# State-space layer with adapters: two sums of the readout handed to accumulating DMAs, the last step of softplus to VectorE

## The chip, the cores and the metric

One core of one Trainium2 chip runs the whole program. The metric is the device time of one execution in microseconds; lower is better.

## The reference

Eight samples of 256 tokens and 1,024 features pass through one layer, float32 throughout:

```python
x = x + attn(cond(x))        # cond: x W + b + 2 * (x A[slot]) B[slot], one adapter per sample
x = x + ffn(cond2(x))        # ffn: top 2 of 8 experts of rank 64
# attn, D = 2048 channels, N = 16 states
u, gate = split(h @ W_in.T)
u = silu(causal_conv4(u) + conv_b)
dt, Bm, Cm = rmsnorm of split(u @ Wx.T)           # 64, 16 and 16 wide
delta = softplus(dt @ Wdt.T + dt_bias)
state = exp(delta * A) * state + (delta * u) * Bm  # a scan over 256 tokens, per channel and state
y = sum over the 16 states of state * Cm + u * D
out = (y * silu(gate)) @ W_out.T
```

## The kernel before

The work is cut into `CHUNKS` = 128 chunks. Chunk `i` is sample `b = i // 16` and block `c = i % 16` of 128 channels; channels lie on the partitions, tokens along the free dimension. The 16 states of a chunk are taken in four quarters `q` of four states, so that one quarter is a plane of 128x1024 elements. Each engine has its own in-order program, and the engines meet at semaphores only.

For a chunk `i` the work is this:

- GpSimd forms `w = delta * u` (`weight`, 128x256) and from it the four input planes `w * Bm` (`dbu(i, q)`, 128x1024 each) into the ring `st` of state buffers, one chunk ahead of VectorE.
- ScalarE forms the four decay planes (`decay(i, q)`, four Exp of 128x255 each) in one of two PSUM tiles, `Tps[q % 2]`. It may begin one only when VectorE has multiplied the plane that was there (`mul_done`).
- VectorE scans each plane in place (`scan(i, q)`, line 1303) and multiplies it by `Cm` (`mul(i, q)`). Products 0, 2 and 3 go to `st` (line 1315). Product 1 stays in PSUM (line 1313), and `add_first` (line 1320) adds product 0 to it and writes `st`.
- GpSimd adds product 1 into product 2 (`add(i, 2)`), that into product 3 (`add(i, 3)`, both line 1538), and folds the four states of the result into two (`fold`, line 1544, 128x512).
- TensorE sums the two that are left with an identity matrix (`sum_states`, line 655) into `gbank`, VectorE adds `u * D` (`y_sum`, line 1326) and multiplies by the gate (`y_gate`, line 1331).

Beside this each chunk has up to four TensorE jobs from fixed tables: `late_job` (bank `late`: output projection of the sample before, experts), `small_job` (bank `small`: projections of `delta`, called "dt", logits and others), `half_job` (half of `gbank`: the adapter layer two samples ahead, part of the experts) and `end_job` (the first dt job of the next sample, at c = 13, in `late`). Within chunk `i` TensorE runs late job, small job, `sum_states(i-1)`, half job, end job, then waits in `ubank_free` for ScalarE's silu of the gate (`q_done`), and then runs the u projection 20 chunks ahead and the gate projection of chunk `i+1` (lines 611 and 638). A job waits until its bank was emptied. The silu waits for the three convolution taps that VectorE runs after `scan(i, 2)` (line 1284). `y_sum(i-1)` stands in VectorE's program of chunk `i`, and waits for `sum_states(i-1)` and for the half job of chunk `i`, which shares the bank.

Softplus is `relu(z) + ln(1 + exp(-|z|))` for two chunks at a time (128x512, 64 times in all). ScalarE empties the bank in two passes, Relu into `delta` (line 1016) and Abs into `tmp` (line 1017), which frees the bank; then it runs Exp and Ln on `tmp` (lines 1023, 1025); GpSimd adds `tmp` to `delta` (`delta_add`, line 1548).

Weights come in tiles of 512 KB through a ring of six buffers, issued by SyncE (line 489).

## Time and profile before

| | us |
|---|---|
| median of 3 runs (2444.42 to 2445.68) | 2444.53 |
| the profiled execution | 2442.7 |
| its span, from first to last instruction | 2440.9 |
| TensorE busy | 2240.2 (92%) |
| VectorE busy | 2229.0 (91%) |
| GpSimd busy | 2116.4 (87%) |
| ScalarE busy | 1614.2 (66%) |

"Busy" is the time in which an engine had an instruction under way. The profiled execution lies 1.8 us above its span and 1.8 us below the median. The granted TensorE clock was 0.96 of full speed over the span.

### The profile page before, as it was taken

Reading aid. Unit: us, or ns where it says so; the run is one execution under the profiler, and the core shown is the slowest. Engines: PE = TensorE matmul, PEld = TensorE weight load, DVE = VectorE, ACT = ScalarE, POOL = GpSimd, SP = SyncE. Lnnn points to the kernel's source line nnn. Section 1 sums busy time; section 2 is a strip of 40 time slices with the busy share of each in tenths; the row PEclk is TensorE's granted clock in tenths of the full one; section 3 lists DMA queues with packets and bytes.
Section 4 is the critical chain, followed back from the end, with each engine's and each line's share of the span. In section 5 each row is a group of like instructions: output and inputs, shape, how many; then the busy total and the mean of one; then the engine's idle time right before and its main releaser. Section 6 shows DMA issues by size and latency. Waiting matters only on the chain.

```text
span 2440.9 us, 30553 instructions
## 1 busy us (share of the span) xinstructions
PE 2240.2 (92%) x10140; PEld 1900.0 (78%) x10140; DVE 2229.0 (91%) x2104; ACT 1614.2 (66%) x3763; POOL 2116.4 (87%) x1090
## 2 busy tenths in 40 slices
PE   8989999999899998999989999999989977787879
PEld 7777878888678877888868887788878765666767
DVE  1389999999999999999999999999999999998892
ACT  1467667776777667776677667776677666765550
POOL 0189889999999999999899999999899999999870
PEclk9999999999999999999989998999999998989989
DMA  7454445444454444544455433644345332632342
GB/s 227 143 202 109 139 137 172 150 138 132 125 191 154 147 139 158 165 147 139 136 168 161 148 130 118 208 159 136 117 165 161 122 108 70 202 104 96 112 139 97
DMA packets 133178, 352.15 MB, mean 144 GB/s; under 512 B 38733, under 2 KB 43341, under 8 KB 131549
## 3 DMA queue, kind: packets, MB, share of 16 engines
q1 hardware_dynamic: 110254, 298.28, 37.9%
q10 hardware_dynamic: 22768, 51.93, 6.2%
q8 instruction: 81, 1.33, 0.2%
q14 instruction: 75, 0.61, 0.1%
HBM read 339.14 MB, written 11.02 MB: 143 GB/s over the span
## 4 chain that ended last, share of the span: by engine, by line
PE 42%; POOL 22%; DVE 21%; issue 9%; ACT 6%; DMA 1%; ACTq 0%; SPq 0%; DVEq 0%; POOLq 0%
POOL st L1530 12%; DVE scan L1303 11%; PE late L692 8%; PE ubank L638 7%; PE ubank L611 7%; POOL st L1538 6%; PE gbank L590 3%; DVE st L1315 3%; DVE ubank L1284 2%; PE scan L611 2%; DVE scan L1313 2%; ACT L1223 2%; POOL st L1544 2%; ACT scan L1133 2%; PE gbank L655 2%
## 5 line engine op out<-in xcount | busy, mean ns | idle before, releaser
L1530 POOL TENSOR_TENSOR st<-w_sb,bc 128x1024 f32<-128x1024 f32 x512 | 1198.0, 2357 | 122.7 <-PE gbank L655 110.3
L1303 DVE TENSOR_TENSOR_SCAN scan<-scan,st 128x1024 f32<-128x1024 f32 x512 | 1167.5, 2288 | 33.9 <-ACT scan L1133 18.4
L1133 ACT ACTIVATE scan<-delta,A_sb 128x255 f32<-128x255 f32 x2048 | 846.1, 459 | 0.1
L1538 POOL TENSOR_TENSOR st<-st 128x1024 f32<-128x1024 f32 x255 | 601.1, 2357 | 20.8 <-DVE st L1315 10.8
L611 PE MATMUL ubank<-h,wt 128*128 128x256 f32 x1712 | 423.3, 404 | 93.1 <-ACT qg L1223 87.6
L638 PE MATMUL ubank<-h,wt 128*128 128x256 f32 x2048 | 471.2, 384 | 23.2 <-ACT qg L1223 23.2
L611 PEld LDWEIGHTS ubank<-h,wt 128*128 128x128 f32 x1712 | 345.2, 204 | 161.8 <-ACT qg L1223 109.2
L638 PEld LDWEIGHTS ubank<-h,wt 128*128 128x128 f32 x2048 | 393.6, 193 | 81.7 <-ACT qg L1223 27.2
L1315 DVE TENSOR_TENSOR st<-scan,bc 128x1024 f32<-128x1024 f32 x384 | 453.8, 1208 | 0.0
L692 PE MATMUL late<-yg,wt 128*128 128x256 f32 x1792 | 407.1, 386 | 26.3 <-DVE x L1340 22.1
L1130 ACT ACTIVATE scan<-iota 128x4 f32<-128x4 f32 x512 | 86.9, 170 | 491.7 <-DVE st L1315 455.9
L692 PEld LDWEIGHTS late<-yg,wt 128*128 128x128 f32 x1792 | 347.2, 194 | 78.4 <-DVE x L1340 24.9
L1223 ACT ACT_TABLE_LOAD x128 | 164.2, 1283 | 171.9 <-DVE ubank L1284 163.7
L1548 POOL TENSOR_TENSOR delta<-delta,tmp 128x512 f32<-128x512 f32 x64 | 81.3, 1270 | 113.3 <-ACT tmp L1025 113.3
L1544 POOL TENSOR_TENSOR st<-st 128x512 f32<-128x512 f32 x127 | 161.5, 1271 | 10.0
L1137 ACT ACT_TABLE_LOAD x129 | 165.5, 1283 | 2.4
L1284 DVE SCALAR_TENSOR_TENSOR ubank<-up,cw,ubank 128x256 f32<-128x256 f32 x321 | 154.6, 482 | 9.3 <-DVE wf L1405 1.5
L1320 DVE TENSOR_TENSOR st<-scan,st 128x1024 f32<-128x1024 f32 x128 | 156.6, 1223 | 4.1
L655 PE MATMUL gbank<-st,ident 128*128 128x256 f32 x508 | 137.6, 394 | 22.5 <-POOL st L1544 16.0
L1313 DVE TENSOR_TENSOR scan<-scan,bc 128x1024 f32<-128x1024 f32 x128 | 156.2, 1220 | 0.3 <-DMA bc<-bc_rows 0.3
L590 PE MATMUL gbank<-xb,wt 128*128 128x256 f32 x672 | 153.6, 382 | 0.2 <-ACT h L976 0.2
L590 PEld LDWEIGHTS gbank<-xb,wt 128*128 128x128 f32 x672 | 128.7, 192 | 18.5 <-ACT h L976 0.6
(219 smaller groups left out, 2257.1 us busy)
## 6 DMA issues: line engine op xcount, KB each, us to landing
wt<-in_W_in SPq DMA_DIRECT2D x256, 512.0 KB, 3.6
wt<-in_W_out SPq DMA_DIRECT2D x132, 512.0 KB, 3.4
wt<-in_cond_W SPq DMA_DIRECT2D x64, 512.0 KB, 3.6
bc<-bc_rows ACTq DMA_DIRECT2D x64, 512.0 KB, 6.8
wt<-G_tiles SPq DMA_DIRECT2D x32, 512.0 KB, 3.6
wt<-in_ffn_B SPq DMA_DIRECT2D x20, 512.0 KB, 3.6
xb<-in_x SPq DMA_DIRECT2D x8, 1024.0 KB, 7.1
x<-in_x ACTq DMA_DIRECT2D x28, 256.0 KB, 4.0
```

Source lines behind the costliest of these rows:

```text
L590: mm(o, wt[:, n % W_RING, k, :], xb[:, k, :], start=(k == 0), stop=False)
L611: last = mm(o[:, 0:T], wt[:, n % W_RING, k, :], h0[:, b % 3, k, :], start=(k == 0), stop=(k == KH - 1))
L638: last = mm(ubank[:, T:2 * T], wt[:, n % W_RING, k, :], h0[:, b % 3, k, :], start=(k == 0), stop=(k == KH - 1))
L692: last = mm(o, wt[:, n % W_RING, k, :], yg[:, (NC * f + h * KH + k) % Y_RING, :], start=(h == 0 and k == 0), stop=(h == 1 and k == KH - 1))
L1133: last = fn(t[:, k, 1:T], delta[:, c, 1:T], ACT.Exp, scale=A_sb[:, col:col + 1])
L1223: fn(qg[:, i % 2, :], ubank[:, T:2 * T], ACT.Silu).then_inc(q_done, 1)
L1303: v_.tensor_tensor_scan(Tps[q % 2][:, :], Tps[q % 2][:, :], x_, 0.0, ALU.mult, ALU.add).then_inc(scan_done, 1)
L1313: v_.tensor_tensor(Tps[1][:, :], Tps[1][:, :], cq, ALU.mult).then_inc(prod_done, 1)
L1315: v_.tensor_tensor(plane(n), Tps[q % 2][:, :], cq, ALU.mult).then_inc(mul_done, 1)
L1530: tt(st[:, n % ST_RING, :, :], w_sb[:, i % 2:i % 2 + 1, :].to_broadcast([P, NQ, T]), bc[:, 0, q * NQ:(q + 1) * NQ, :], ALU.mult).then_inc( ...
L1538: tt(st[:, n % ST_RING, :, :], st[:, n % ST_RING, :, :], st[:, (n - 1) % ST_RING, :, :], ALU.add).then_inc(add_done, 1)
L1544: tt(t[:, 0:2, :], t[:, 0:2, :], t[:, 2:4, :], ALU.add).then_inc(add_done, 1)
```

## The change

The readout's sums. Product 1 goes to `st` like the others, and `add_first` and `add(i, 3)` go. In their place stand two DMAs that GpSimd issues (`add_dma`): one adds plane 0 into plane 1, the other plane 2 (which by then holds the sum of three) into plane 3. `add(i)`, the sum of plane 1 into plane 2, stays on GpSimd. The ring `st` has 8 buffers instead of 6. VectorE's order changes to scan 0, mul 0, scan 1, mul 1, scan 2, taps, mul 2, scan 3, `y_sum`, `y_gate`, mul 3.

Softplus. ScalarE runs Abs from the bank into `delta`, then Exp and Ln in place; VectorE's `delta_sum` computes `max(z, 0) + delta` from the bank in one instruction, and frees the bank. Relu on ScalarE, `delta_add` on GpSimd and the buffer `tmp` go.

For space, the matrix `sel` goes (an expert's weights are spread over partitions by two matmuls with a broadcast column of the identity, 64 partitions each, instead of one with `sel`), and `wT` shares the buffer `la`.

```diff
-ST_RING = 6
+ST_RING = 8
...
-                return mm(o, sel[:, m * P:(m + 1) * P], wT[:, :], start=True, stop=True)
+                for e in range(2):
+                    pick = ident[0:E, 2 * m + e:2 * m + e + 1].to_broadcast([E, ER])
+                    last = mm(o[e * ER:(e + 1) * ER, :], pick, wT[:, :], start=True, stop=True)
+                return last
...
+            def delta_sum(b, j):
+                job = ("dt", b, j)
+                n = 8 * b + j
+                d = delta[:, 2 * j:2 * j + 2, :].rearrange("p c t -> p (c t)")
+                dve.wait_ge(sp_step, 3 * n + 3)
+                v_.scalar_tensor_tensor(d, home(job)[:, :], 0.0, d, ALU.max, ALU.add).then_inc(delta_done, 1)
+                dve.wait_ge(delta_done, n + 1)
+                dve.sem_inc(ev_inc(job), 1)
...
                 scan(i, 0)
                 if i:
                     take_late(i - 1)
+                mul(i, 0)
                 scan(i, 1)
+                for n, j in softplus_of(i):
+                    delta_sum(n, j)
                 if i:
                     take_rest(i - 1)
-                mul(i, 0)
                 mul(i, 1)
-                add_first(i)
                 scan(i, 2)
...
+                mul(i, 2)
                 if c == 13 and b < LAST:
                     norm(b + 1)
                 scan(i, 3)
-                mul(i, 2)
-                mul(i, 3)
...
                     y_sum(i - 1)
                     y_gate(i - 1)
+                mul(i, 3)
...
             def dbu(i, q):
-                if q == 2 and i:
-                    pool.wait_ge(mul_done, 4 * i - 2)
-                if q == 1 and i >= 2:
+                if q == 3 and i >= 2:
                     pool.wait_ge(id_mm, i - 1)
...
+            def add_dma(i, k):
+                n = 4 * i + k
+                pool.wait_ge(mul_done, n + 1)
+                if k == 3:
+                    pool.wait_ge(add_done, 2 * i + 1)
+                pool.dma_start(st[:, n % ST_RING, :, :], st[:, (n - 1) % ST_RING, :, :], accum_op=ALU.add
+                               ).then_inc(acc_st[k // 2], 16)
+
+            def add(i):
+                n = 4 * i + 2
+                pool.wait_ge(acc_st[0], 16 * (i + 1))
+                pool.wait_ge(mul_done, n + 1)
...
             def fold(i):
-                pool.wait_ge(add_done, 3 * i + 2)
+                pool.wait_ge(acc_st[1], 16 * (i + 1))
...
             for i in range(CHUNKS):
-                for b, j in softplus_of(i - 1):
-                    delta_add(b, j)
-                if i + 1 < CHUNKS:
+                last = i + 1 == CHUNKS
+                if not last:
                     weight(i + 1)
-                    for q in range(3):
-                        dbu(i + 1, q)
-                add(i, 2)
-                if i + 1 < CHUNKS:
-                    add(i, 3)
-                    fold(i)
+                    dbu(i + 1, 0)
+                    dbu(i + 1, 1)
+                if i:
+                    fold(i - 1)
+                add_dma(i, 1)
+                if not last:
+                    dbu(i + 1, 2)
                     dbu(i + 1, 3)
+                add(i)
+                if not last:
+                    add_dma(i, 3)
```

The steps of the experts' softmax, which stand between these at one chunk of each sample, are left out here; they keep their order.

## Rows read from the trace of the kernel before

**Rows 1.** The page, busy time, share of the span and instructions by engine.
```profile
PE 2240.2 (92%) x10140; PEld 1900.0 (78%) x10140; DVE 2229.0 (91%) x2104; ACT 1614.2 (66%) x3763; POOL 2116.4 (87%) x1090
```

**Rows 2.** Windows: length, busy us of PE, PEld, DVE, ACT, POOL; clock; DMA.
```profile
193.00:305.00 112.00, 108.89 (x493) 94.27 (x492) 106.04 (x93) 81.83 (x195) 100.67 (x53) 0.98 0.43 122
1000.40:1194.00 193.60, 190.35 (x885) 164.77 (x884) 190.10 (x185) 133.71 (x314) 182.66 (x96) 0.99 0.47 149
1194.00:1281.60 87.60, 77.59 (x340) 64.09 (x339) 86.69 (x78) 66.20 (x154) 82.12 (x42) 0.92 0.47 154
1830.00:2106.30 276.30, 231.54 (x1001) 192.87 (x1002) 272.31 (x251) 194.29 (x448) 261.58 (x135) 0.92 0.39 127
2106.29:2227.00 120.71, 96.46 (x390) 80.24 (x389) 111.61 (x87) 80.31 (x181) 119.06 (x63) 0.90 0.36 119
```

**Rows 3.** Line 1303, the scans: ns min/median/max, first and last start; one releaser.
```profile
L1303 DVE TENSOR_TENSOR_SCAN scan<-scan,st x512: 2271/2289/2299, 119.7 to 2377.4; 128x1024 f32<-128x1024 f32 x171
...
  DVE xs L1290: 1.3, 6
```

**Rows 4.** Timeline of VectorE: start us, us, instruction.
```profile
1015.47 1.23 DVE L1313 TENSOR_TENSOR scan<-scan,bc 128x1024 f32<-128x1024 f32 x1
1016.73 1.23 DVE L1320 TENSOR_TENSOR st<-scan,st 128x1024 f32<-128x1024 f32 x1
1017.87 2.29 DVE L1303 TENSOR_TENSOR_SCAN scan<-scan,st 128x1024 f32<-128x1024 f32 x1
```

**Rows 5.** Groups of instructions: xcount, busy us, mean ns, idle before and releasers.
```profile
L1284 DVE SCALAR_TENSOR_TENSOR ubank<-up,cw,ubank 128x256 f32<-128x256 f32 x321 | 154.6, 482 | 9.3 <-DVE wf L1405 1.5 <-ACT ubank L991 0.3
L1349 DVE TENSOR_TENSOR x<-x,late 128x512 f32<-128x512 f32 x14 | 9.4, 673 | 0.0
L1016 ACT ACTIVATE delta<-small 128x512 f32<-128x512 f32 x63 | 36.3, 577 | 3.0 <-ACT hw L1095 1.5 <-issue 1.5
L1548 POOL TENSOR_TENSOR delta<-delta,tmp 128x512 f32<-128x512 f32 x64 | 81.3, 1270 | 113.3 <-ACT tmp L1025 113.3
```

**Rows 6.** Timeline of GpSimd at the start of sample 7, one chunk.
```profile
2107.36 0.73 POOL L1517 TENSOR_TENSOR w_sb<-delta,u_sb 128x256 f32<-128x256 f32 x1
2108.17 6.98 POOL L1530 TENSOR_TENSOR st<-w_sb,bc 128x1024 f32<-128x1024 f32 x3
2115.11 4.79 POOL L1538 TENSOR_TENSOR st<-st 128x1024 f32<-128x1024 f32 x2
2119.98 1.26 POOL L1544 TENSOR_TENSOR st<-st 128x512 f32<-128x512 f32 x1
2121.20 2.35 POOL L1530 TENSOR_TENSOR st<-w_sb,bc 128x1024 f32<-128x1024 f32 x1
2124.74 0.73 POOL L1517 TENSOR_TENSOR w_sb<-delta,u_sb 128x256 f32<-128x256 f32 x1
```

**Rows 7.** DMA: the SyncE queue (packets, MB, share), issues with KB and us to landing.
```profile
q1 hardware_dynamic: 110254, 298.28, 37.9%
...
wt<-in_W_in SPq DMA_DIRECT2D x256, 512.0 KB, 3.6
...
bc<-bc_rows ACTq DMA_DIRECT2D x64, 512.0 KB, 6.8
...
h<-in_x SPq DMA_DIRECT2D x1, 1024.0 KB, 6.5
```

**Rows 8.** Timeline of ScalarE's queue, three DMA issues in a row.
```profile
1240.99 1.52 ACTq L1033 DMA_DIRECT2D bc<-bc_rows  x3
```

**Rows 9.** Waits: who waited for whom, us in total, times, longest us.
```profile
POOL st L1530 <- PE gbank L655: 110.3, 49, 9.5
```

**Rows 10.** Timeline of TensorE: a heavy chunk, then c = 14 of sample 3.
```profile
1022.10 1.03 PE L655 MATMUL gbank<-st,ident 128*128 128x256 f32 x4
...
1224.25 1.13 PE L749 MATMUL late<-wT,sel 8*128 8x256 f32 x4
...
1234.51 5.17 PE L611 MATMUL ubank<-h,wt 128*128 128x256 f32 x16 [3.40 <-ACT qg L1223]
```

More of the change, by code:

```diff
@@ L219, in build @@
           A_mat, D_par, W_out, base_W, base_b, lora2_A, lora2_B, GT_all, ffn_B,
-          ident_in, mean_in, sel_in, iota_in, out):
+          ident_in, mean_in, iota_in, out):
     with ExitStack() as ctx:
@@ L376, in build @@
         scan_done = sem("scan_done")
-        prod_done = sem("prod_done")
         mul_done = sem("mul_done")
         add_done = sem("add_done")
+        acc_st = [sem(f"acc_st{i}") for i in range(2)]
         id_mm = sem("id_mm")
@@ L395, in build @@
         block = ctx.enter_context(nc.Block())
-        N_CONSTS = 12
+        N_CONSTS = 11
         SOFT_STEPS = 10
@@ L1074, in evac @@
                     ms_evac(job)
-                elif kind == "dt":
-                    dt_evac(job)
                 elif kind == "la2":
@@ L1084, in evac @@
                     act.wait_ge(*made(job))
+                    if b + 3 < B:
+                        act.wait_ge(*made(("cond", b + 3, 7)))
                     fn(wT[:, :], o[0:E, 0:T], ACT.Copy).then_inc(ev_inc(job), 1)
@@ L1177, in _ @@
                     for prev in (late_job(i - 1), small_job(i - 1), end_job(i - 1)):
-                        if prev and prev[0] not in ("wout", "wb", "B", "lg", "ms"):
+                        if prev and prev[0] not in ("wout", "wb", "B", "lg", "ms", "dt"):
                             evac(prev, i)
@@ L1311, in mul @@
                 cq = bc[:, 1, q * NQ:(q + 1) * NQ, :].rearrange("p n t -> p (n t)")
-                if q == 1:
-                    v_.tensor_tensor(Tps[1][:, :], Tps[1][:, :], cq, ALU.mult).then_inc(prod_done, 1)
-                else:
-                    v_.tensor_tensor(plane(n), Tps[q % 2][:, :], cq, ALU.mult).then_inc(mul_done, 1)
-            def add_first(i):
-                dve.wait_ge(prod_done, i + 1)
-                dve.wait_ge(mul_done, 4 * i + 1)
-                v_.tensor_tensor(plane(4 * i + 1), Tps[1][:, :], plane(4 * i), ALU.add).then_inc(mul_done, 1)
+                v_.tensor_tensor(plane(n), Tps[q % 2][:, :], cq, ALU.mult).then_inc(mul_done, 1)
             def y_sum(i):
@@ L1422, in _ @@
             norm(0)
+            delta_sum(0, 0)
+            delta_sum(0, 1)
             def take_late(i):
@@ L1459, in _ @@
                     soft_max_step(b - 1, 3)
-                add_first(i)
+                scan(i, 2)
                 if weigh:
                     soft_max_step(b - 1, 4)
-                scan(i, 2)
-                if weigh:
-                    soft_max_step(b - 1, 5)
                 if i:
@@ L1469, in _ @@
                             conv_tap(v, k)
+                if weigh:
+                    soft_max_step(b - 1, 5)
+                mul(i, 2)
                 if c == 13 and b < LAST:
@@ L1472, in _ @@
                 scan(i, 3)
-                if i == CHUNKS - 1:
-                    y_sum(i - 1)
-                    y_gate(i - 1)
-                mul(i, 2)
                 if b and c == 10:
                     soft_max_in(b - 1)
-                mul(i, 3)
-                if i and i < CHUNKS - 1:
+                if i:
                     if i == NC - 1:
@@ L1531, in dbu @@
                    bc[:, 0, q * NQ:(q + 1) * NQ, :], ALU.mult).then_inc(dbu_done, 1)
-            def add(i, k):
+            def add_dma(i, k):
                 n = 4 * i + k
+                pool.wait_ge(mul_done, n + 1)
                 if k == 3:
-                    pool.wait_ge(add_done, 3 * i + 1)
+                    pool.wait_ge(add_done, 2 * i + 1)
[4 more added lines that the diff above has]
+                pool.wait_ge(acc_st[0], 16 * (i + 1))
                 pool.wait_ge(mul_done, n + 1)
@@ L1542, in fold @@
                 t = st[:, (4 * i + 3) % ST_RING, :, :]
-                pool.wait_ge(add_done, 3 * i + 2)
+                pool.wait_ge(acc_st[1], 16 * (i + 1))
                 tt(t[:, 0:2, :], t[:, 0:2, :], t[:, 2:4, :], ALU.add).then_inc(add_done, 1)
-            def delta_add(b, j):
-                pool.wait_ge(sp_step, 2 * (8 * b + j) + 2)
-                tt(delta[:, 2 * j:2 * j + 2, :], delta[:, 2 * j:2 * j + 2, :], tmp[:, j % 2, :, :], ALU.add
-                   ).then_inc(dadd_done, 1)
-            delta_add(0, 0)
             weight(0)
-            dbu(0, 0)
-            delta_add(0, 1)
-            for q in range(1, Q):
+            for q in range(Q):
                 dbu(0, q)
             for i in range(CHUNKS):
-                for b, j in softplus_of(i - 1):
-                    delta_add(b, j)
-                if i + 1 < CHUNKS:
+                last = i + 1 == CHUNKS
+                if not last:
                     weight(i + 1)
-                    for q in range(3):
-                        dbu(i + 1, q)
-                add(i, 2)
-                if i + 1 < CHUNKS:
-                    add(i, 3)
-                    fold(i)
+                    dbu(i + 1, 0)
+                    dbu(i + 1, 1)
+                if i:
+                    fold(i - 1)
+                add_dma(i, 1)
+                if not last:
+                    dbu(i + 1, 2)
                     dbu(i + 1, 3)
+                add(i)
+                if not last:
+                    add_dma(i, 3)
 def kernel(**inputs):
```

41 lines of the change are left out of this document (14 added, 27 removed).

## The prediction

> **What bounds the kernel now.** I began with the page's busy shares [rows 1]. No engine is the bound by its average: TensorE has 92%, VectorE 91%, GpSimd 87%. So a gain must be read from each stage. The scans run from 119.7 to 2377.4 us [rows 3]; the last of them is the fourth of its chunk, some 10 us into it, so a chunk takes (2257.7 - 10) / 127 = 17.7 us on average. The windows then split the samples [rows 2]:
>
> - Chunks 1 to 11 of sample 3 (second row) stand for samples 1 to 5: 193.6 us, 17.6 a chunk, TensorE busy 190.35 (98%), VectorE 190.10 (98%). Both are full. There is no room for a gain of more than 193.6 - 190.35 = 3.3 us unless TensorE gets less work.
> - Its chunks 12 to 15 and the next chunk 0 (third row): 87.6 us, VectorE busy 86.69, TensorE 77.59. VectorE is the bound.
> - Chunks 4 to 9 of sample 0 (first row): TensorE 108.89 of 112.0, VectorE 106.04. TensorE is the bound.
> - Sample 6 (fourth row), which has no adapter layer to compute ahead: VectorE 272.31 of 276.3, TensorE 231.54. VectorE is the bound.
> - The first seven chunks of sample 7 (fifth row): GpSimd 119.06 of 120.71, VectorE 111.61. GpSimd is the bound, and one of its chunks takes 2124.74 - 2107.36 = 17.38 us [rows 6].
>
> **VectorE's part.** Product 1 and `add_first` take 1017.87 - 1015.47 = 2.40 us from start to the next scan; one product alone takes 1.14 (1017.87 - 1016.73) [rows 4]. So 1.26 us go per chunk, 161 in all. What comes is `delta_sum`, 64 times. It is not in the trace: from below, a two-operand pass over 128x512 takes 0.67; from above, two of the three-operand passes over 128x256 take 0.96 [rows 5]. I take 0.75, near the pass of equal size. It also waits for its own end before it frees the bank; the same pattern in `norm` left VectorE idle 1.3 / 6 = 0.22 us [rows 3]. So 0.97 each, 62 in all. Net, a sample of 16 chunks and 8 sums loses 20.2 - 7.8 = 12.4 us of VectorE. The new order puts a scan between a product and the decay plane that needs its PSUM tile, so ScalarE is asked for nothing sooner; ScalarE also loses one pass of 0.577 per dt job [rows 5], with 34% of idle time around it, worth nothing by itself.
>
> **GpSimd's part.** It loses one add of two, (2119.98 - 2115.11) / 2 = 2.43 us, per chunk [rows 6], and `delta_add`, 1.27 [rows 5], in half of the chunks. It gains two DMA issues. No DMA of GpSimd is in the trace, and none that accumulates. The issue: from below 0.5 us, what one costs on ScalarE's queue (1.52 / 3) [rows 8]; from above 1.27, a 128x512 pass of GpSimd. I take 1.0, nearer to the engine's own instruction, since software must build the descriptors. A chunk with a dt job is then 17.38 - 1.27 - 2.43 + 2.0 = 15.7 us, if no DMA is late.
>
> **When a DMA is late.** This decides the case. GpSimd is in order. Behind the first DMA stand two input planes, then `add`, which waits for it: cover 2 x 6.94 / 3 = 4.63 us. Behind the second stand `weight` (0.81) and two planes: cover 5.44, then `fold` [rows 6]. If both are late the cycle is add 2.43 + fold 1.22 + 2 x (issue + landing). The landing of a DMA that adds 512 KB in SBUF: from below 3.6 us, a weight tile of 512 KB; from above 6.8 (a broadcast of 512 KB), and nearly the same 6.5 for 1,024 KB [rows 7]. I work out a value between: the queue moved 298.28 MB in 37.9% of 16 engines' span, 20.1 GB/s each, so 512 KB are 1.6 us of movement and 2.0 of fixed time. An add must read both operands and write one; with reading as the limit movement is 3.25, so 5.2 us. Then the first is late by 0.6, the second is covered, and the cycle is 16.3 us, below the 17.4 to 17.7 of now. Hidden, then, but by little: the cycle reaches 17.7 when issue and landing together make 7.0, that is at a landing of 6.0.
>
> The Trainium skill bears on this price. Its page "Collectives: The Full Stack", section "The bandwidth ceiling: the fold count and why AG ≠ RS ≠ AR", says that the adder in the DMA path costs nothing by itself and that a reduction halves the rate because it reads two sources; with that the sum stays as it is. Its page "DMA: Bandwidth & Descriptors", section "Anatomy of one DMA — SWDGE (gpsimd) path", gives a fixed 2.0 us plus bytes at 436 GB/s; with two reads this makes an estimate of 4.4 us, both DMAs covered, and a cycle of 15.7. Our own rows give a slower movement, since the weight tiles share the engines. No run here yet shows an accumulating DMA.
>
> **The other edits.** `dbu(i+1, 3)` now waits for `sum_states(i-1)`, only one issue and one plane after the fold. GpSimd already lost 110.3 us to that wait [rows 9], and in a heavy chunk TensorE comes to it late, at 1022.10 [rows 10]. Behind it is `add`. But the loop from one such sum to the next is plane 2.31 + add 2.43 + issue 1.0 + cover 5.44 + fold 1.22 + sum 1.0 = 13.4, below 17.6: the wait moves and is not longer. Without that cover it would cost what the loop exceeds the chunk. The bank of a dt job is freed by VectorE two scans (2.2 each), a product and the sum into the chunk, 6.5 us, where ScalarE's two passes did it. Behind a late bank stand TensorE's late job and all after it. It matters at c = 14, where the bank `late` is wanted at 1224.25; some 3 us later fall into the 3.40 that TensorE waits there for the silu anyway [rows 10]. Elsewhere 6.9 us of output projection come first. The doubled matmuls for the experts' weights are 8 instructions more per sample, 190.35 / 885 = 0.215 each, 1.7 us, in the stretch where TensorE has 10 us idle [rows 2]. `y_sum(i-1)` now comes one product earlier, so TensorE's half job has less time before VectorE waits for it; in the heavy chunks I give back 1 of the 3.3 us or more for that. `wT` in `la` changes no order. The weight tiles: the accumulating DMAs add 256 x 3.25 us, 34% of the span, to engines that the SyncE queue alone keeps busy for 37.9% [rows 7]; with six buffers the tiles are asked for about a chunk and a half ahead, so I book 5 us in all.
>
> **The sum.** Samples 1 to 5: the light stretch loses 5 x 1.26 - 3 x 0.97 = 3.4, the heavy one 1, so 4.4 each, 22. Sample 0: 3. Sample 6: 12, the full net of VectorE. Sample 7: seven chunks from 17.38 to 16.3, 7.5; the rest, where TensorE and VectorE wait for each other, 4.5; so 12. Together 49, less 5 for the weight tiles: 44 us. 2442.7 - 44 = 2398.7 for the profiled execution; the median of the runs lay 1.8 above it, so **2400 us**.
>
> **Rivals.**
> - *Most of it stays hidden, my forecast*, 42%. Its own range is 2370 to 2437: the lower end with both DMAs covered and the heavy stretch at TensorE's 190.35, the upper with a landing of 5.9.
> - *The adding DMAs are late and GpSimd becomes the bound (slower than before).* From a landing of 6.0 on, each 0.1 us costs 0.2 x 128 = 26 us. At the row of the broadcast (6.8) and an issue of 1.0 the cycle is 3.65 + 15.6 = 19.25, and 128 x (19.25 - 17.7) = 198, so 2643 us; with an issue of 1.27 it is 2712. For it: 1,024 KB took 6.5, and both queues' landings lengthen when transfers collide, which the new ones do with the load of SyncE's queue, 298.28 / 128 = 2.3 MB per chunk. Against: half of that movement never leaves SBUF. 38%. The Trainium skill, the same DMA page, section "Issuing engines are not separate DMA queues", speaks for this side.
> - *No change*: the light stretches lose to the later bank and the later fold what VectorE gains, and only samples 6 and 7 stay, less some stalls: 2445 us, 10%.
> - *A larger gain*: TensorE's idle time in the light stretches takes up its backlog of the heavy ones, so samples 1 to 5 fall to TensorE's own 190.35 + 77.59 + 1.7 = 269.6 of 281.2, 11.6 each: 2400 - 5 x 7.2 = 2364 us, 10%.
>
> **Chances.** Faster by over 0.2% (5 us, about what a measurement of this kernel can tell): 42 + 10 less the edge, 50%. Within it 10%. Slower 40%, the late DMAs and a rest for an issue that is dearer than any row here. The range runs from 2350, under the larger gain, to 2650, the broadcast's landing; beyond it I leave about 2 in 10, nearly all above.
>
> **What would show it.** VectorE busy near 2229 - 99 = 2130 us, GpSimd's adds halved, and the time from a DMA issue of GpSimd to its landing. At 5.2 the waits of `add` for a DMA are about 0.6 each and those of `fold` none; TensorE stays at 98% in the heavy chunks. If the DMAs are late, `add` and `fold` have large waits on DMA, VectorE waits at its scans for input planes, and the cycle of GpSimd equals the chunk. The forecast is wrong if issue and landing exceed 7.0 together, or if TensorE's wait for the bank of a dt job shows in the chain.

## The result and the profile after

| | before | after |
|---|---|---|
| median of the runs, us | 2444.97 (2444.42 to 2445.68, 4 runs) | 2473.99 (2471.33 to 2479.27, 4 runs) |
| the profiled execution, us | 2442.7 | 2471.33 |
| its span, us | 2440.9 | 2469.5 |

The ratio of the medians is 1.0123, 95% interval [1.0111, 1.0135]: the change costs 29 us. The forecast was 2400.

The page's busy times of the changed kernel, which answer to [rows 1]:

```profile
PE 2249.7 (91%) x10204; PEld 1900.4 (77%) x10204; DVE 2135.8 (86%) x2040; ACT 1600.9 (65%) x3699; POOL 1970.8 (80%) x1154
```

VectorE does 93 us less and GpSimd 146 us less than before, and the kernel is slower. No engine is busier than 91%, so the engines wait for one another. The chain of work that ended last, as a share of the span, has moved to GpSimd and its DMAs (first line before, the others after):

```profile
PE 42%; POOL 22%; DVE 21%; issue 9%; ACT 6%; DMA 1%; ACTq 0%; SPq 0%; DVEq 0%; POOLq 0%
POOL 45%; PE 23%; DMA 13%; issue 9%; DVE 8%; ACT 2%; POOLq 0%; SPq 0%; ACTq 0%; DVEq 0%
POOL st L1522 25%; DMA st<-st 11%; POOL st L1538 8%; POOL st L1531 5%; POOL st L1544 5%; DVE scan L1304 4%; PE ubank L636 3%; PE ubank L609 2%; PE scan L609 2%; PE late L690 2%; POOL w_sb L1510 2%; DMA bc<-bc_rows 2%; DVE st L1313 2%; PE gbank L588 2%; PE gbank L653 1%
```
Which engines wait is in the groups of instructions. Columns: count, busy us, mean ns of one, then the idle time before them and what ended it.

```profile
L1522 POOL TENSOR_TENSOR st<-w_sb,bc 128x1024 f32<-128x1024 f32 x512 | 1234.7, 2469 | 138.2 <-PE gbank L653 80.9
...
L1538 POOL TENSOR_TENSOR st<-st 128x1024 f32<-128x1024 f32 x128 | 314.8, 2459 | 37.0 <-DMA st<-st 36.9
L1531 POOL DMA_DIRECT2D st<-st x255 | 223.8, 878 | 113.2 <-DVE st L1313 58.9
...
L653 PE MATMUL gbank<-st,ident 128*128 128x256 f32 x508 | 156.5, 436 | 148.1 <-POOL st L1544 141.9
...
L1544 POOL TENSOR_TENSOR st<-st 128x512 f32<-128x512 f32 x127 | 161.3, 1270 | 43.0 <-DMA st<-st 42.7
```

The DMA lines and the issues with their median time to landing, of the same kernel (compare [rows 7]):

```profile
q1 hardware_dynamic: 110238, 298.27, 36.2%
q0 software_dynamic: 36720, 133.71, 30.0%
...
wt<-in_W_in SPq DMA_DIRECT2D x256, 512.0 KB, 4.3
st<-st POOLq DMA_DIRECT2D x255, 512.0 KB, 5.3
...
bc<-bc_rows ACTq DMA_DIRECT2D x64, 512.0 KB, 8.8
...
xb<-in_x SPq DMA_DIRECT2D x8, 1024.0 KB, 7.9
```

Behind the median of 5.3 us stands a wide spread, for the adding DMAs alone (line 1531):

```profile
DMA to landing us min/median/max: 4.4/5.3/11.4
```

The waits of the same kernel, who for whom: us in total, times, longest.

```profile
PE gbank L653 <- POOL st L1544: 141.9, 37, 9.0
POOL st L1522 <- PE gbank L653: 80.9, 49, 7.2
...
POOL st L1531 <- POOL st L1538: 53.8, 80, 0.8
DVE gbank L1319 <- PE gbank L731: 49.2, 10, 8.8
POOL st L1522 <- DMA bc<-bc_rows: 47.5, 10, 9.7
POOL st L1544 <- DMA st<-st: 42.7, 26, 4.8
POOL st L1538 <- DMA st<-st: 36.9, 22, 6.6
```

The same waits before:

```profile
POOL st L1538 <- DVE st L1315: 10.8, 4, 7.9
PE gbank L655 <- POOL st L1544: 16.0, 11, 4.0
POOL st L1530 <- DMA bc<-bc_rows: 1.7, 2, 1.5
```

Two waits have grown. TensorE waits for the fold 141.9 us where it waited 16.0, in 37 places of up to 9 us: few and long. And GpSimd waits 47.5 us, ten times, for the rows of `Bm` of the next sample.

**Where the time went.** The starts of the first scan of each chunk give the length of every chunk. Worked out from the start times of the scans (us; c is the chunk's block):

```
sample 3, c = 0 to 15
before 17.8 17.8 17.5 18.5 17.2 17.1 17.2 17.2 18.1 17.2 17.3 19.4 16.8 18.1 16.8 17.4
after  17.3 17.3 17.1 18.9 16.7 17.8 16.0 17.8 18.6 16.7 16.3 18.5 16.2 17.0 20.7 24.3

c = 14 and 15 of samples 0 to 6
before 16.8 16.8  16.8 17.4  16.8 17.4  16.8 17.4  16.8 17.4  16.8 17.4  15.7 16.2
after  16.6 23.8  21.3 22.6  20.7 24.2  20.7 24.3  21.3 23.7  16.5 22.5  16.1 24.6
```

The last two chunks of samples 0 to 6 take 298.9 us where they took 236.7: 62.2 more. All the rest is 33.6 us shorter. The sum is the 28.6 by which the span grew. The windows show it for sample 3. First row chunks 0 to 13, second row chunks 14 and 15, of the changed kernel:

```profile
999.29:1241.49 242.20, 236.86 (x1107) 203.78 (x1107) 231.45 (x224) 172.19 (x398) 212.39 (x126) 1.00 0.77 207
1241.49:1286.54 45.05, 30.61 (x132) 23.47 (x131) 33.33 (x30) 26.37 (x60) 34.34 (x20) 0.77 0.72 204
```

and the same chunks before:

```profile
973.79:1220.76 246.97, 240.02 (x1106) 207.20 (x1105) 242.84 (x232) 172.75 (x405) 231.17 (x119) 0.99 0.46 148
1220.76:1255.01 34.25, 27.93 (x123) 21.84 (x122) 33.97 (x31) 27.19 (x64) 33.64 (x19) 0.90 0.52 177
```

In chunks 0 to 13 TensorE stays at 98%, and they are 4.8 us shorter. The forecast was 4.4 for the whole sample, most of it in chunks 12 to 15 and 0; chunks 1 to 11 alone gave 2.5 where 1 was forecast. In chunks 14 and 15 every engine idles for 10.7 us or more of 45. TensorE's granted clock is 0.77 of full speed there on average, 0.90 before. After TensorE had stood idle for 7.00 us it is 0.50, the lower of its two levels (1.2 GHz, from 1256.10 to 1258.20), and four matmuls at line 653 take 2.08 us there; at 2.4 GHz they take 1.03.

The timeline of GpSimd around the two chunks of the changed kernel, from chunk 12 on (start, us, instruction, in brackets the idle time before it and what ended it):

```profile
1208.91 0.88 POOL L1531 DMA_DIRECT2D st<-st  x1 [0.63 <-DVE st L1313]
...
1220.12 1.26 POOL L1544 TENSOR_TENSOR st<-st 128x512 f32<-128x512 f32 x1 [4.82 <-DMA st<-st]
...
1236.49 1.27 POOL L1544 TENSOR_TENSOR st<-st 128x512 f32<-128x512 f32 x1
1237.70 0.87 POOL L1531 DMA_DIRECT2D st<-st  x1
1238.31 4.97 POOL L1522 TENSOR_TENSOR st<-w_sb,bc 128x1024 f32<-128x1024 f32 x2
1245.54 2.35 POOL L1538 TENSOR_TENSOR st<-st 128x1024 f32<-128x1024 f32 x1 [2.26 <-DMA st<-st]
1248.52 0.88 POOL L1531 DMA_DIRECT2D st<-st  x1 [0.63 <-POOL st L1538]
...
1254.85 1.26 POOL L1544 TENSOR_TENSOR st<-st 128x512 f32<-128x512 f32 x1
...
1265.17 1.05 POOL L1510 TENSOR_TENSOR w_sb<-delta,u_sb 128x256 f32<-128x256 f32 x1
1273.03 4.65 POOL L1522 TENSOR_TENSOR st<-w_sb,bc 128x1024 f32<-128x1024 f32 x2 [6.81 <-DMA bc<-bc_rows]
1277.63 1.26 POOL L1544 TENSOR_TENSOR st<-st 128x512 f32<-128x512 f32 x1
```

and of the other engines, with SyncE's queue at the first three lines:

```profile
1207.29 0.65 SPq L490 DMA_DIRECT2D xb<-in_x  x1
...
1238.14 0.33 SPq L487 DMA_DIRECT2D wt<-in_ffn_B  x1
1238.51 0.43 SPq L485 DMA_DIRECT2D wt<-in_ffn_B  x1
...
1256.16 2.08 PE L653 MATMUL gbank<-st,ident 128*128 128x256 f32 x4 [7.00 <-POOL st L1544]
...
1278.95 2.08 PE L653 MATMUL gbank<-st,ident 128*128 128x256 f32 x4 [7.16 <-POOL st L1544]
...
1284.55 0.49 DVE L1319 SCALAR_TENSOR_TENSOR gbank<-u_sb,D_sb,gbank 128x256 f32<-128x256 f32 x1 [7.20 <-PE gbank L731]
```

There are two different late folds.

- *c = 15.* GpSimd forms the planes of the next sample's first chunk ahead of the fold of chunk 14. They need the new rows of `Bm`, whose loads ScalarE issues in chunk 15. GpSimd stands for 6.81 us at them; the fold behind comes at 1277.63, TensorE idles 7.16, the half job comes later, and VectorE idles 7.20 at `y_sum`. Before, the fold of chunk 14 was done when GpSimd came to those planes, and they waited 1.7 us in all.
- *c = 14.* The first adding DMA is issued at 1237.70, and two weight tiles 0.4 and 0.8 us later. The add that needs it waits 2.26 and begins 7.84 us after the issue, where the median landing is 5.3, and the whole cycle from issue to issue (1256.05 in the full timeline) takes 18.35 us. The fold comes at 1254.85, and TensorE has idled 7.00 us when it can sum. In samples 1 to 4 chunk 14 is 3.8 to 4.5 us longer, in samples 0, 5 and 6 at most 0.4.

The 2.26 us are less than a third of those 7.00; the lateness began in chunk 12. At 1207.29 SyncE issues the load of `x` for a later sample (1 MB), and 1.6 us behind it GpSimd issues its second adding DMA, which the fold awaits until 1220.12, 11.2 us after the issue. In samples 1 to 4 that wait is 4.3 to 4.8 us and the one of the add behind it 2.0 to 2.5. In samples 5 and 6 there is no such load of `x`, in sample 0 it falls between two adding DMAs, and in these three samples `add` and `fold` wait at most 1.1 us for DMAs in chunks 12 to 14.

### The profile page after: what moved, and what is told of

The parts are those of the page before. It is cut to its first block, busy times and chain, and to the rows that moved or that the text cites. A ratio compares the mean times of both kernels' runs of the same rounds, so it can differ in the third digit from the quotient of the medians.

```text
span 2469.5 us, 30616 instructions
## 1 busy us (share of the span) xinstructions
PE 2249.7 (91%) x10204; PEld 1900.4 (77%) x10204; DVE 2135.8 (86%) x2040; ACT 1600.9 (65%) x3699; POOL 1970.8 (80%) x1154
## 3 DMA queue, kind: packets, MB, share of 16 engines
q1 hardware_dynamic: 110238, 298.27, 36.2%
q0 software_dynamic: 36720, 133.71, 30.0%
## 4 chain that ended last, share of the span: by engine, by line
POOL 45%; PE 23%; DMA 13%; issue 9%; DVE 8%; ACT 2%; POOLq 0%; SPq 0%; ACTq 0%; DVEq 0%
POOL st L1522 25%; DMA st<-st 11%; POOL st L1538 8%; POOL st L1531 5%; POOL st L1544 5%; DVE scan L1304 4%; PE ubank L636 3%; PE ubank L609 2%; PE scan L609 2%; PE late L690 2%; POOL w_sb L1510 2%; DMA bc<-bc_rows 2%; DVE st L1313 2%; PE gbank L588 2%; PE gbank L653 1%
## 5 line engine op out<-in xcount | busy, mean ns | idle before, releaser
L1522 POOL TENSOR_TENSOR st<-w_sb,bc 128x1024 f32<-128x1024 f32 x512 | 1234.7, 2469 | 138.2 <-PE gbank L653 80.9
L1304 DVE TENSOR_TENSOR_SCAN scan<-scan,st 128x1024 f32<-128x1024 f32 x512 | 1171.3, 2288 | 20.9 <-ACT scan L1127 15.9
L1313 DVE TENSOR_TENSOR st<-scan,bc 128x1024 f32<-128x1024 f32 x512 | 623.9, 1219 | 13.8 <-DVE wf L1398 2.1
L636 PE MATMUL ubank<-h,wt 128*128 128x256 f32 x2048 | 476.5, 387 | 5.2 <-ACT qg L1215 5.2
L609 PE MATMUL ubank<-h,wt 128*128 128x256 f32 x1712 | 405.3, 391 | 23.1 <-ACT qg L1215 19.7
L690 PE MATMUL late<-yg,wt 128*128 128x256 f32 x1792 | 398.2, 380 | 10.6 <-DVE x L1333 7.3
L1538 POOL TENSOR_TENSOR st<-st 128x1024 f32<-128x1024 f32 x128 | 314.8, 2459 | 37.0 <-DMA st<-st 36.9
L1531 POOL DMA_DIRECT2D st<-st x255 | 223.8, 878 | 113.2 <-DVE st L1313 58.9
L653 PE MATMUL gbank<-st,ident 128*128 128x256 f32 x508 | 156.5, 436 | 148.1 <-POOL st L1544 141.9
L653 PEld LDWEIGHTS gbank<-st,ident 128*128 128x128 f32 x508 | 102.8, 212 | 180.1 <-POOL st L1544 160.9
L1510 POOL TENSOR_TENSOR w_sb<-delta,u_sb 128x256 f32<-128x256 f32 x128 | 132.4, 1035 | 113.5 <-DVE delta L1292 113.5
L1544 POOL TENSOR_TENSOR st<-st 128x512 f32<-128x512 f32 x127 | 161.3, 1270 | 43.0 <-DMA st<-st 42.7
L1319 DVE SCALAR_TENSOR_TENSOR gbank<-u_sb,D_sb,gbank 128x256 f32<-128x256 f32 x128 | 61.2, 478 | 138.1 <-PE gbank L592 55.6
```

The costliest lines, as they stand in the source:

```text
L609: last = mm(o[:, 0:T], wt[:, n % W_RING, k, :], h0[:, b % 3, k, :], start=(k == 0), stop=(k == KH - 1))
L636: last = mm(ubank[:, T:2 * T], wt[:, n % W_RING, k, :], h0[:, b % 3, k, :], start=(k == 0), stop=(k == KH - 1))
L653: last = mm(gbank[:, 0:T], ident[:, :], st[:, n % ST_RING, k, :], start=(k == 0), stop=(k == 1))
L690: last = mm(o, wt[:, n % W_RING, k, :], yg[:, (NC * f + h * KH + k) % Y_RING, :], start=(h == 0 and k == 0), stop=(h == 1 and k == KH - 1))
L1304: v_.tensor_tensor_scan(Tps[q % 2][:, :], Tps[q % 2][:, :], x_, 0.0, ALU.mult, ALU.add).then_inc(scan_done, 1)
L1313: v_.tensor_tensor(plane(n), Tps[q % 2][:, :], cq, ALU.mult).then_inc(mul_done, 1)
```

## The experiments

Two theories stood at the start. **A, the boundary:** the loss sits at the wait for the rows of `Bm` (c = 15) and at one late loop (c = 14). **B, the DMAs:** they load the DMA engines and GpSimd's queue everywhere, and the boundary is only where it is seen. All times of kernels are medians; the kernel before had 2443.9 to 2445.0 beside each. Chunk lengths and waits come from the one profiled execution of a kernel. In the changed kernel, `e3_rows_early`, `e4_no_add_dmas`, `e6_edge_order` and `e10_ring9_rows` it was the fastest of the runs, by 3 to 18 us under the median.

### Taking one suspect away

`e1_rows_once`: the row loads of `Bm` happen for sample 0 only.

```diff
+                if b:
+                    return
...
-                if c == 0:
-                    pool.wait_ge(B_ld[q], 16 * (b + 1))
+                if i == 0:
+                    pool.wait_ge(B_ld[q], 16)
```

> Leaves out the reload of the rows of Bm for samples 1 to 7 (the rows of sample 0 serve for all), so GpSimd never waits for them. Theory A (the changed order of GpSimd puts the wait for the next sample's rows ahead of the fold of chunk 14, and TensorE's sum stands behind it): chunk 15 of a sample falls from 23.7 us on average to about 17.5, so 7 x 6.2 = 43 us, 2474 to about 2431; the second chunk that became longer, 14, stays at 20.7. Theory B (the accumulating DMAs slow all other transfers, and the rows are only one of them): chunk 15 falls by the little that the four loads take from the other transfers, under 2 us each, so 2460 or more.

Measured: 2434.06 us (2426.74 to 2443.91), ratio to before 0.9955 [0.9942, 0.9969], 40 us under the changed kernel. Chunk 15 fell to 16.5 to 17.2 in samples 0 to 5 and to 19.7 in sample 6. Chunk 14 still had 20.9 and 21.3 in two samples. That is theory A's forecast (2431) within 3 us. But the edit takes away two things, the wait and 28 of the 64 loads of `bc`, which land in 5.8 us at the median instead of 8.8; the 40 us are both together.

`e4_no_add_dmas`: both accumulating DMAs are left out; `add` and `fold` wait for VectorE's products alone.

```diff
-                pool.dma_start(st[:, n % ST_RING, :, :], st[:, (n - 1) % ST_RING, :, :], accum_op=ALU.add
-                               ).then_inc(acc_st[k // 2], 16)
```

> Leaves out both accumulating DMAs (two of the three sums of a chunk), with all else in place. Theory A: 255 issues of 0.88 us and the waits for them go from GpSimd, which is off the bound in the middle of a sample, so the chunks 0 to 13 change by less than 0.3 us each; chunk 15 keeps most of its wait for the rows (over 5 us of 6.8): 2440 to 2455. Theory B: the rows and weight tiles land as fast as before the change, chunk 15 falls to 18, and the whole to about 2400.

Measured: 2426.39 us (2421.83 to 2432.84), 0.9934 [0.9917, 0.995]. Chunk 14 is 16.5 in every sample, and chunk 15 still 19.4 to 22.0. Its waits, the fold at line 1541 here:

```profile
POOL st L1522 <- DMA bc<-bc_rows: 57.5, 15, 7.6
...
PE gbank L653 <- POOL st L1541: 48.9, 19, 6.6
```

The time lies between the two forecasts, A's 2440 to 2455 and B's 2400. The lateness at c = 14 belongs to the DMAs. Chunk 15, 45.8 us longer than before over the seven samples in the changed kernel, is still 26.5 longer here; that part goes with the new order of GpSimd's program, which is the same. The DMAs cost 48 us in all. Between the two profiled executions 38 of 49.5 us lie in the last two chunks of samples 0 to 6 and 13 in sample 7; in the other chunks the gain is nothing, as A said. The other loads land faster too (a `W_in` tile in 3.6 us again, not 4.3). Taking away either suspect gives back more than the whole loss of 29 us, so the two aren't parts that add up.

### Curing c = 15 by order

`e2_fold_ahead` puts the fold of chunk 14 ahead of the planes of the next sample.

```diff
+                edge = i % NC == NC - 1
+                if edge:
+                    fold(i - 1)
+                if not last:
                     dbu(i + 1, 0)
                     dbu(i + 1, 1)
-                if i:
+                if i and not edge:
```

> Only at the last chunk of a sample GpSimd folds chunk 14 before it asks for the next sample's rows. Theory A: the sum of TensorE no longer stands behind the rows; GpSimd still waits for them, but it is a chunk ahead of VectorE, so chunk 15 falls from 23.7 to 18 to 19.5 us, 30 to 40 us in all: 2434 to 2444. Theory B: no change, 2470 to 2478.

Measured: 2487.99 us (2481.45 to 2499.92), 1.0178 [1.0142, 1.0215]. It is slower still, which neither theory forecast: chunk 15 fell to 17.0 to 19.8 in samples 0 to 5, but the chunk 0 that follows rose to 20.7 to 28.1. GpSimd's timeline of this kernel shows why:

```profile
1279.97 1.04 POOL L1510 TENSOR_TENSOR w_sb<-delta,u_sb 128x256 f32<-128x256 f32 x1
1286.87 1.26 POOL L1544 TENSOR_TENSOR st<-st 128x512 f32<-128x512 f32 x1 [5.86 <-DMA st<-st]
```

The two planes had been the cover of the second DMA's landing. Without them the fold waits 5.86 us for the DMA instead of 6.81 for the rows, and those planes come later as well.

`e3_rows_early` issues the first two row loads at the end of chunk 14, ahead of their use.

```diff
-                    for q in range(3):
-                        load_B(b + 1, q)
+                    load_B(b + 1, 2)
...
+                if c == 14 and b < LAST:
+                    for q in range(2):
+                        load_B(b + 1, q)
```

> ScalarE issues the loads of the first two quarters of the next sample's rows at the end of its chunk 14 instead of in its chunk 15, some 8 us earlier. Theory A: the wait of 6.8 us for the rows goes nearly altogether, 2430 to 2440. Theory B: 2465 or more, since the rows land late wherever they are issued.

Measured: 2469.26 us (2460.43 to 2470.98), 1.0102 [1.0086, 1.0119]. A's forecast missed, and the time is in B's range. The wait for rows fell from 47.5 to 12.5 us, but the fold's wait for its DMA rose from 42.7 to 57.8. Chunk 15 fell to 16.5 to 19.5 in four samples and stayed at 22.1 to 22.6 in three. So the wait for the rows by itself, with all loads kept, was worth only 4.7 us here. `e6_edge_order` puts, at the boundary, the fold and the first DMA ahead of the two planes that wait for the rows, and the other two planes behind the second DMA, with the early rows:

> At the last chunk of a sample GpSimd first folds, issues the first DMA and only then makes the two planes that wait for the next sample's rows, and the other two after its second DMA, which they cover; two of the four row loads are issued a chunk earlier. Theory A: neither the rows nor an uncovered landing stands ahead of a sum of TensorE for more than 1 or 2 us: chunk 15 falls from 23.7 to about 18 and chunk 0 stays below 19, 2474 less 30 to 40 is 2434 to 2444. Theory B: the landings of the colliding DMAs, 8 us each, remain, and chunks 15 and 0 together stay above 40 us: 2460 or more.

Measured: 2488.23 us (2470.7 to 2497.52), 1.0197 [1.0179, 1.0216]. A's forecast missed; the time is in B's range, though chunks 15 and 0 together stayed under 40 us. In the profiled execution, at 2470.7 the fastest, the fold waited 90.8 us for its DMA, and chunk 1 took 20.4 to 23.2. Each of the three took a wait away and got another a little later.

### Curing c = 14 by a buffer

`e5_ring9`: nine state buffers. Now the first plane of chunk i waits for the sum of chunk i-3, where the fourth waited for that of i-2. Five weight buffers make room.

```diff
-W_RING = 6
+W_RING = 5
-ST_RING = 8
+ST_RING = 9
...
-                if q == 3 and i >= 2:
-                    pool.wait_ge(id_mm, i - 1)
+                if q == 0 and i >= 3:
+                    pool.wait_ge(id_mm, i - 2)
```

> Nine state buffers, and five weight buffers instead of six for the space. The plane that had to wait for TensorE's sum of the chunk before last now waits for a sum a whole chunk older. Theory A (the chunks at the end of a sample are long because of a loop: TensorE's sum, late in a heavy chunk, releases the fourth input plane, behind which stand add, second DMA, fold, and the next sum, which a light chunk wants early): chunk 14 of samples 1 to 4 falls from 20.9 to about 17 us, chunk 15 keeps the wait for the rows, 23; 2474 less 16 to 30 is 2444 to 2458. Theory B (only the collision of the DMAs with the load of x, at chunk 13, and of the rows, at 15, matters): chunk 14 stays above 20, 2470 or more.

Measured: 2456.08 us (2452.85 to 2458.89), 1.0044 [1.0028, 1.0061]. That is within A's forecast, and so is the fall of chunk 14. Chunk 14 is 16.5 in samples 0 to 5 and 15.2 in sample 6; chunk 15 still 21.4 to 24.8. `e12_weights5` is the five weight buffers alone (the first pair of lines of the diff):

> The changed kernel with five weight buffers instead of six, a control for the runs that need the space. The tiles are asked for a chunk and more ahead; nearly no cost: 2472 to 2480. If the weight tiles are short with the accumulating DMAs in their way: 2490 or more.

Measured: 2462.87 us (2458.02 to 2470.47), 1.0063 [1.0046, 1.008]. That is 11 us less than with six, which no forecast had. The ninth state buffer with its later wait is thus worth 6.8 us, not 18, and with four runs of each kernel, whose ranges touch, even that is barely clear of the noise.

What the ninth buffer does at c = 14 the traces show better than the times. Add up, in chunks 12 to 14 of a sample, what `add` and `fold` wait for DMAs. In the eight traces of kernels with eight state buffers and the new softplus (the changed kernel, `e1`, `e2`, `e3`, `e6`, `e12`, `e14`, `e15`), where that sum is at most 1.4 us chunk 14 takes 15.2 to 17.2; from 2.2 to 3.9 us it takes 17.2 to 19.4; from 4.6 us on 20.0 to 21.6. With nine state buffers it is 16.5 even where the sum is 5.0 (sample 0 of `e5_ring9` and of `e10_ring9_rows`).

`e7_ring9_edge` is the nine buffers with the order of `e6_edge_order`:

> Both edits together. Theory A: chunks 14, 15 and 0 take 17, 18 and 18 us, so only the gain of the other chunks is left, 2410 to 2420, below the kernel before. Theory B: 2455 or more.

Measured: 2477.29 us (2466.05 to 2479.51), 1.0119 [1.0094, 1.0144]. A's forecast missed, B's held. Chunk 14 is 16.5 or less in all but one sample, but `add` waits 83.5 us for DMAs and the fold 78.0, and chunks 0 to 2 take 17 to 23 each.

`e9_inline_edge` has nine buffers and early rows, and in the last two chunks of samples 0 to 6 GpSimd makes the second sum itself, where the fold would wait for a DMA.

```diff
+            def add_third(i):
+                n = 4 * i + 3
+                pool.wait_ge(mul_done, n + 1)
+                pool.wait_ge(add_done, 2 * i + 1)
+                tt(st[:, n % ST_RING, :, :], st[:, n % ST_RING, :, :], st[:, (n - 1) % ST_RING, :, :], ALU.add
+                   ).then_inc(third_done, 1)
```

> Nine state and five weight buffers, two row loads a chunk earlier, and for the last two chunks of samples 0 to 6 the second sum and the fold are done by GpSimd's own adds at once (2.4 us instead of issue and landing); at the last chunk the first DMA is issued ahead of the planes that wait for the rows. Theory A (it is the landing, 8 us where other transfers collide, standing ahead of TensorE's sum, that makes the last two chunks and the first long): chunks 14, 15 and 0 take 16.5, 17 to 18.5 and 17.5 to 19 us; 2474 less 18 (chunk 14) less 35 to 40: 2415 to 2425, below the kernel before. Theory B (GpSimd's lack of time at the boundary, rows or not): GpSimd gets 3 us more to do there, and the chunks stay at 22: 2450 or more.

Measured: 2443.87 us (2436.45 to 2455.29), 0.9994 [0.9979, 1.0009]. The time lies between the forecasts. Chunks 14, 15 and 0 came out at 16.5, 17.0 and 17.3 in most samples, as A expected, but one or two of chunks 1 to 3 rose to 20 to 28 in samples 1 to 7. GpSimd does 2.4 us more in each of the two chunks; that it pays for this a little later is argued, not shown.

`e10_ring9_rows` is `e5_ring9` with the early rows of `e3_rows_early`, and nothing else.

> The kernel with nine state buffers (2456) plus the two early row loads. Theory A: chunk 15 falls from 22.8 to about 20, since the wait for the rows goes but the second DMA of chunk 14 still lands in 8 us or more: 2456 less 15 to 20, 2436 to 2441. If the wait for the rows alone made it long: 17, 2416. If the early loads only collide sooner: 2456.

Measured: **2431.59 us** (2424.5 to 2440.54, 8 runs), 0.9956 [0.9942, 0.997]: faster than both kernels. Chunk 15 came out as it should if the wait for the rows alone made it long (17), the time between that forecast (2416) and A's (2436 to 2441). Its waits:

```profile
PE gbank L653 <- POOL st L1546: 83.9, 33, 6.9
...
POOL st L1540 <- DMA st<-st: 39.4, 25, 6.6
...
POOL st L1546 <- DMA st<-st: 33.6, 38, 3.6
POOL st L1524 <- DMA bc<-bc_rows: 30.3, 7, 6.6
```

TensorE waits for the fold 83.9 us instead of 141.9. Chunk 15 of samples 0 to 5 is 16.5 to 17.2, and 21.3 in sample 6. What is left sits in chunk 0, 19.2 to 22.2 in samples 1 to 7 where before has 16.8 to 17.8. GpSimd's timeline of this kernel at its start:

```profile
1257.30 2.36 POOL L1524 TENSOR_TENSOR st<-w_sb,bc 128x1024 f32<-128x1024 f32 x1 [6.31 <-DMA bc<-bc_rows]
```

It is the fourth plane that now waits for its rows, and the fold isn't behind it but ahead.

`e14_rows_weights5` is the same with eight state buffers:

> The changed kernel with the first two row loads at the end of chunk 14 and five weight buffers, still eight state buffers. Theory A (the gains add up, and the ninth state buffer gives its own 7 us): 2436 to 2446 us. Rival B (the early rows need the ninth buffer, since without it the late loop of chunk 14 sits where the rows land): 2452 to 2465 us.

Measured: 2444.28 us (2439.26 to 2451.42), 1.0007 [0.9996, 1.0018], in A's range. So there is a ladder: 2473.99, with five weight buffers 2462.87, with early rows too 2444.28, with the ninth state buffer 2431.59. The steps don't add up in another order: early rows gave 4.7 us with six weight buffers and 18.6 with five, the ninth buffer 6.8 without early rows and 12.7 with them.

### The weight buffers

`e13_before_weights5` is the kernel before with five of them, `e15_weights4` the changed kernel with four.

> The kernel before with five weight buffers in place of six, nothing else. Theory A (fewer weight tiles in flight collide less with the accumulating DMAs; the kernel before has none): no change, 2440 to 2450 us. Rival B (six buffers are too many for any kernel of this order, whatever adds the products): 2430 to 2438 us.

Measured: 2444.74 us, 1.0002 [0.9993, 1.0011], as A said; one of its 11 runs took 5929 us, which nothing here explains.

> The changed kernel with four weight buffers. Theory A (fewer weight tiles in flight leave the accumulating DMAs free): between 2450 and 2462 us, and the landing of a weight tile under 4.3 us. Rival B (only the places at which a tile's load falls changed with the ring, by luck): anything from 2455 to 2500 us, with TensorE waiting for weight tiles.

Measured: 2497.97 us (2481.99 to 2500.37), 1.0208 [1.0181, 1.0235]. A's forecast missed; the time is in B's range, but without the waits for weights that B named. The kernel without accumulating DMAs doesn't notice a buffer less; the changed one goes from 2474 to 2463 to 2498 with six, five and four. There is no trend, a `W_in` tile lands no sooner (4.3, 4.2, 4.7), and with four TensorE waits 164.8 us for the fold and under 3 us for weights. Which accumulating DMA is hit by a weight tile depends on when the tile's buffer comes free; that this luck is the whole difference is argued, not shown. One place is seen: the wait of the fold for its DMA beside the load of `x` (3.4 to 5.0 us in samples 1 to 4) stands in all five traces with eight state and six weight buffers that keep the DMAs. With five (`e12_weights5`) `add` and `fold` wait at most 1.2 us in chunk 12, and chunk 14 is 17.2 or less in samples 1 and 3. But the profiled executions with six and five buffers have nearly one span, 2469.5 and 2468.7 us, since other chunks lost what chunks 14 and 15 gained, so they don't explain the 11 us.

### Each half of the change alone

`e8_softplus_only` is the kernel before with the new softplus; the products are added as before.

> The kernel before with the new softplus alone. The price of one sum on VectorE was taken as 0.97 us, and VectorE was held to be full in samples 1 to 6. If both hold: 8 x 0.97 x 6 = 47 us more there, less about 8 in the first seven chunks of sample 7, where GpSimd loses its 1.27 us in five of them: 2444.5 + 39, some 2475 to 2485. If VectorE had slack, as in the heavy chunks where TensorE was also full, only the light stretches pay: 5 x 2.9 + 8 = 22 less 8, 2455 to 2460.

Measured: 2481.55 us (2479.32 to 2484.22), 1.0154 [1.0137, 1.0171], as expected. The busy times of this kernel:

```profile
PE 2249.3 (91%) x10140; PEld 1902.8 (77%) x10140; DVE 2272.6 (92%) x2168; ACT 1583.3 (64%) x3699; POOL 2039.3 (82%) x1026
```

VectorE has 44 us more, and the kernel 37: it was full, as [rows 2] show. `e11_dmas_only` is the changed kernel with the old softplus (and five weight buffers, since `tmp` needs the room).

> The changed kernel with the old softplus (Relu on ScalarE, the sum on GpSimd), and five weight buffers for the space. VectorE has 62 us less to do, GpSimd 81 more. If VectorE is the bound in the light chunks: 2.9 us less per sample there, 15 to 20 in all, but GpSimd's cycle with a sum is 16.3 + 1.3 = 17.6 and delays the folds at the boundary by 1.3 each: 2474 less 5, give or take 10. If the softplus part costs here what it costs alone (37 us): 2437.

Measured: 2509.77 us (2506.87 to 2528.08), 1.0285 [1.0243, 1.0326]. Both forecasts, some 2469 and 2437, missed. Here TensorE waits for the fold 188.9 us in 59 places, where `e12_weights5` has 139.0 in 42. So the softplus on VectorE costs 37 us alone and gives 46.9 us beside the DMAs (2509.77 - 2462.87). The reading, argued from the order of GpSimd's program: with the products added by DMA VectorE has room, and GpSimd's 1.27 us of `delta_add` stands in front of the late fold.

## Why the prediction was wrong

The sign was wrong; the time lies inside the range. Step by step:

- **VectorE's part** was right: busy 2135.8 against 2130. `delta_sum` takes 0.67 us, not 0.75.
- **The issue** on GpSimd has a row of 0.88 us. The next instruction begins 0.61 after its start (1237.70 to 1238.31) and is 0.3 longer, so 0.9 in all, near the 1.0 taken. But of the 127 second issues, which stand right behind `add`, 80 also wait 0.62 to 0.76 us for it, 53.8 us in all, and 50 issues wait 58.9 us for VectorE's products. The sum had neither.
- **The landing** is 5.3 us as the median, 5.2 was taken. The waits of `add` on a DMA were forecast at 0.6 for each of 128; they are 36.9 us in 22 places of up to 6.6. The fold, said to wait for none, waits 42.7. The median was right and the spread decided: 4.4 to 11.4 us, 7.84 beside two weight tiles, 11.2 beside the load of `x`. The Trainium skill's page "DMA: Bandwidth & Descriptors", section "Anatomy of one DMA — SWDGE (gpsimd) path", gave the estimate of 4.4; the trace has 5.3 at the median and 4.4 as the shortest, so the rows served better. The same page of the Trainium skill, section "Issuing engines are not separate DMA queues", has it that DMAs of all issuers share the same 16 engines. The trace agrees: the loads of the other queues lengthened from 3.6 to 4.3 and from 6.8 to 8.8.
- **The inner chunks** were right where the load is heavy. Chunks 0 to 13 of samples 1 to 5 are 17 us shorter in all (22 were forecast for the whole of them), sample 7 is 13 shorter (12). Sample 6 is 6 shorter outside its last two chunks, where 12 were forecast for all of it, and sample 0 is 4 longer there, where 3 less were forecast. The windows that [rows 2] call chunks 1 to 11 and 12 to 0 start about half a chunk late; the balance of the engines in them, which is all that was used, holds.
- **The step that failed** is the overlap under "When a DMA is late", together with a wait that the sum left out, the one for the rows of `Bm`. *The overlap.* It was reckoned with one landing for all DMAs: the first late by 0.6, the second always covered, a cycle of 16.3 us. The cycle for both late, add 2.43, fold 1.22 and twice issue and landing, was the right loop, and its own limit was a landing of 6.0. In sample 3, landings of 11.2 and 7.84 us came within three cycles, which took 20.9, 16.4 and 18.35 us (the last: 7.84 to the landing, add 2.35, wait and issue 1.2, two planes and `weight` 5.7, fold 1.26); samples 1, 2 and 4 are alike, and chunk 14 grew by 3.8 to 4.5 us in all four. TensorE's waits for the fold went from 16.0 to 141.9 us. The loop of 13.4 us from one sum to the next took the cover where a landing can be longer. *The rows.* `dbu(i+1, 0)` at a new sample waits for rows of `Bm`, and the new order puts the fold behind it; the text names what stands behind the wait for `sum_states`, and not behind this one. GpSimd stands 47.5 us at the rows where it stood 1.7, and chunk 15 is 45.8 us longer in all. Without the reload of the rows the kernel is 40 us faster (`e1_rows_once`). The sentence "the wait moves and is not longer" held for the wait it is about: 80.9 us for 110.3. That TensorE also wants the sum earlier in light chunks, so that a fold which suits a heavy chunk is late there, is argued from the order of its jobs.
- **The rival** "the adding DMAs are late and GpSimd becomes the bound" had the sign and 38%, and was in part right. GpSimd (45%) and the adding DMAs (11%) make 56% of the chain that ended last, where GpSimd made 22%. But it was the bound by stretches only: it is busy 80%, VectorE's scans wait for its planes once, 2.8 us, chunks 0 to 13 of samples 1 to 7 are shorter than before, and the price of 198 us was far off. A few late DMAs, each passed on by the fold to TensorE and by the bank to VectorE, were enough.
- **Luck.** The time lies inside the range only because the range reached to 2650 for that rival; the forecast's own range ended at 2437.

Without the 62 us of the two last chunks the kernel would have taken some 2412 us. Shown are the parts of the rows (`e1_rows_once`), of the DMAs (`e4_no_add_dmas`) and of the two halves, and that chunk 14 grows with the waits for DMAs in the chunks before. That the load of `x` delays the DMA beside it rests on where the waits fall; no run moves that load. How much of chunk 15 is the wait for the rows and how much their traffic isn't separated. Open is why five weight buffers are 11 us faster than six.

## What to carry to other kernels

When an operation is moved in an in-order queue, write down for each wait that it passes what now stands behind it, at the boundaries of the outer loop first: a wait that cost nothing because the urgent work was already done costs its full length once that work stands behind it. Hand work to a DMA with cover for its worst landing, not for its median, since here the long landings recurred where another load was issued beside them; a further buffer of the results gives that cover, while a changed order of issue moves the wait elsewhere. And try the halves of a change together and alone: here each alone costs more than both.

## What the runs showed of the hardware

- A 512 KB accumulating DMA from SBUF to SBUF: landing 5.3 us as the median, 4.4 to 11.4 in all, 7.84 beside two weight tiles and 11.2 behind a load of 1 MB. 255 of them took 30.0% of the 16 engines' span for 133.71 MB; the SyncE queue took 36.2% for 298.27 MB, so in this kernel a byte that is added costs the engines 1.85 times one that is loaded.
- After an issue GpSimd's next instruction is longer: `weight` 1.04 against 0.73 us (0.73 again in `e4_no_add_dmas`), the first plane 2.65 against 2.36.
- The doubled matmuls for the experts' weights cost nothing: 8 instructions to two halves of the partitions, each 64 columns of weights, took 1.08 us, where 4 of 128 columns took 1.13 [rows 10].
- The runs of the kernels with the new order spread more: 2424.5 to 2440.54 in eight runs of `e10_ring9_rows`, against 2440.42 to 2445.82 in 21 of the kernel before. It isn't the accumulating DMAs alone, since `e4_no_add_dmas`, without them, has 2421.83 to 2432.84 in four runs.
